# One VectorE operation for the low halves of an expert's weights, GpSimd left with the scatters, SyncE reading its table four values at a time

## The reference

```python
x = hidden_states.reshape(-1, orig_shape[-1])
probs = jax.nn.softmax(x @ gate_w.T, axis=-1)
topk_w, topk_idx = jax.lax.top_k(probs, K)                    # K = 6 of E = 64
topk_w = topk_w / jnp.sum(topk_w, axis=-1, keepdims=True)
combine = jnp.sum(jax.nn.one_hot(topk_idx, E, dtype=x.dtype) * topk_w[..., None], axis=1)
h = jax.nn.silu(jnp.einsum('th,eih->tei', x, experts_w1))     # 256 -> 176
y = jnp.einsum('tei,ehi->teh', h, experts_w2)                 # 176 -> 256
routed_out = jnp.einsum('teh,te->th', y, combine)
...
shared_out = jax.nn.silu(g) * u @ shared_down.T
return (routed_out + shared_out).reshape(orig_shape)
```

## Time and profile before

| | before |
|---|---|
| median of 3 executions | 1873.75 us (1868.09 to 1883.21) |
| the profiled execution | 1885.33 us, of which the span from the first to the last instruction is 1883.4 us |
| TensorE busy | 1558.3 us (83%) |
| VectorE busy | 1331.7 us (71%) |
| ScalarE busy | 922.6 us (49%) |
| GpSimd busy | 911.4 us (48%) |
| mean granted TensorE clock | 0.899 of full speed |
| GpSimd, `outputs<-hsw,x_rows` (L1358) | 160 times, 243.1 us |
| GpSimd, `ew_lo<-ew,ew_hi` (L1294) | 160 times, 154.7 us |
| VectorE, `ew_lo<-ew,ew_hi` (L875) | 160 times, 108.4 us |

### The profile page before, as it was taken

The page is one execution under the profiler, slowest core; times in us unless marked ns, Lnnn a source line. Parts: engine busy times, 40 slices in busy tenths (PEclk is TensorE's granted clock), DMA queues, the critical chain, the costliest instruction groups (busy, mean ns, idle before and its releaser), DMA issues. The chain is left out here.

```text
span 1883.4 us, 33921 instructions
## 1 busy us (share of the span) xinstructions
PE 1558.3 (83%) x9484; PEld 1165.7 (62%) x9484; DVE 1331.7 (71%) x2125; ACT 922.6 (49%) x1696; POOL 911.4 (48%) x714
## 2 busy tenths in 40 slices
PE   6689998699996899986999978716299999999931
PEld 5466665566664666654666648404198888878820
DVE  3568887588886688875888855503567777777767
ACT  3465554555554655546555533101076666666610
POOL 0334433434343444334344410566378999989920
PEclk8799999999998999998999985757599999999965
DMA  4012221022220112210221200334388888888744
GB/s 141 0 43 63 62 67 34 8 64 61 67 58 9 42 59 67 67 33 0 67 67 58 61 3 1 138 117 157 96 252 250 246 245 248 247 241 234 209 165 161
DMA packets 111029, 198.16 MB, mean 105 GB/s; under 512 B 17481, under 2 KB 63063, under 8 KB 110816
## 3 DMA queue, kind: packets, MB, share of 16 engines
q1 hardware_dynamic: 98656, 171.75, 30.9%
q0 software_dynamic: 12288, 25.41, 3.7%
HBM read 160.96 MB, written 44.50 MB: 109 GB/s over the span
## 5 line engine op out<-in xcount | busy, mean ns | idle before, releaser
L1307 POOL TENSOR_TENSOR ssq<-ssq,ysq 128x512 f32<-128x512 f32 x128 | 164.4, 1284 | 460.9 <-ACT ysq L759 460.9
L963 DVE SCALAR_TENSOR_TENSOR e<-bank,scal,e 128x511 f32<-128x511 f32 (+2 forms) x384 | 287.5, 749 | 54.3 <-ACT e L754 18.9
L1358 POOL DMA_INDIRECT outputs<-hsw,x_rows x160 | 243.1, 1519 | 33.3 <-issue 28.5
L461 PE MATMUL bank<-e,wn 128*128 128x512 f32 x512 | 252.8, 617 | 0.0
L386 PE MATMUL bank<-h_hi,wi_hi 128*128 x512 | 237.2, 463 | 18.8 <-POOL wi_lo L1294 14.6
L388 PE MATMUL bank<-h_hi,wi_lo 128*128 x512 | 204.9, 400 | 0.0
L387 PE MATMUL bank<-h_lo,wi_hi 128*128 x512 | 202.2, 395 | 0.0
L875 DVE TENSOR_TENSOR hid_lo_rows<-hid_rows,hid_hi_rows 88x256 fp32r<-88x256 f32 x160 | 120.9, 756 | 113.6 <-ACT hid_hi_rows L705 111.3
L754 ACT ACTIVATE e<-bank,scal 128x512 f32<-128x512 f32 x128 | 99.7, 779 | 199.0 <-PE bank L388 199.0
L1294 POOL TENSOR_TENSOR wi_lo<-wi,wi_hi 128x512 fp32r<-128x512 f32 x128 | 165.5, 1293 | 52.7 <-ACT wi_hi L705 52.7
L386 PE MATMUL bank<-hw_hi,ew_hi 128*88 128x128 f32 x640 | 161.0, 256 | 22.3 <-POOL ew_lo L1294 5.9
(11 more groups left out here) (245 smaller groups left out, 3764.3 us busy)
## 6 DMA issues: line engine op xcount, KB each, us to landing
ew<-expert_w SPq DMA_DIRECT2D x160, 432.0 KB
wi<-in_w SPq DMA_DIRECT2D x128, 256.0 KB, 2.7
x_rows<-grouped SPq DMA_DIRECT2D x160, 130.0 KB
wo<-out_w SPq DMA_DIRECT2D x128, 128.0 KB, 2.4
got<-outputs SPq DMA_DIRECT2D x16, 768.0 KB, 4.3
grouped<-zeros_out SPq DMA_DIRECT2D x65, 130.0 KB
outputs<-hsw,x_rows POOLq DMA_INDIRECT x160
x_all<-x_t SPq DMA_DIRECT2D x4, 512.0 KB, 8.6
```

What stands on the lines that cost most here:

```text
L461: i = mm(p_out[k][:, :], wn[:, par, k * P:(k + 1) * P], y[:, par, :], start=do_out == "first", stop=do_out == "last")
L963: v.scalar_tensor_tensor(dst[:, d:], src[:, 0:SEQ - d], taps(TAPS - 1 - d), dst[:, d:], ALU.mult, ALU.add).then_inc(S[done], 1)
L1307: g_.tensor_tensor(ssq[:, :], ssq[:, :], ysq[:, :], ALU.add).then_inc(S["ssq_done"], 1)
L1358: g_.indirect_dma_start(outputs, bass.IndirectOffsetOnAxis(x_rows[:, i % XD, EMB:EMB + 1].bitcast(U32), 0), y_rows[:, i % YD, :], None, bo ...
```

## The change

Three edits, all around the expert loop.

- VectorE makes the low part of all 864 columns of tile i+1 in one operation (`weights_low`), at the place in its order where it made 512 of them. It signals `w_lo`; the semaphore `w2_lo` is gone, and so is TensorE's wait for it in `second`. Before the loop, `weights_low(0)` comes ahead of `rows_in(0)` and `rows_in(1)` instead of behind them.
- GpSimd's `first_weights` is gone. It issues the 160 scatters, each as soon as its rows are copied.
- SyncE reads four values of a table with one load. In the loop it handles four tiles at a time: eight values are read first, then the transfers are issued. Before tile 4 the order of the first transfers is four loads of rows, then four of weights.

```diff
-            def load_weights(i):
-
-                e = sp.value_load(owner_no[0:1, i:i + 1], min_val=0, max_val=EXPERTS - 1)
+            def load_weights(i, e):
+
                 sp.wait_ge(S["w_lo"], START["w_lo"] + i - 3)
-                sp.wait_ge(S["w2_lo"], START["w2_lo"] + i - 3)
                 sp.dma_start(ew[:, i % DEEP, :], expert_w[bass.ds(e, 1), :, :].rearrange("a p n -> p (a n)"))\
                     .then_inc(S[f"w_in{i % DEEP}"], 16)
...
+            def four(table, i, top):
+
+                return nc.values_load_multi_w_load_instructions(table[0:1, i:i + 4], engines=[mybir.EngineType.SP],
+                                                                min_val=0, max_val=top)[1]
+
             sp.wait_ge(S["fill_rows"], 1)
-            for e in range(EXPERTS):
-                row = sp.value_load(fill_row[0:1, e:e + 1], min_val=0, max_val=SPARE - P)
-                sp.dma_start(grouped_rows[bass.ds(row, P), :], zeros_out[:, :]).then_inc(S["xs_zero"], 16)
+            for e in range(0, EXPERTS, 4):
+                for row in four(fill_row, e, SPARE - P):
+                    sp.dma_start(grouped_rows[bass.ds(row, P), :], zeros_out[:, :]).then_inc(S["xs_zero"], 16)
...
-            for i in range(DEEP, ETILES):
-                load_weights(i)
-                if i + 2 < ETILES:
-                    load_rows(i + 2)
+            early = four(first_row, 0, SPARE)
+            for i in range(DEEP):
+                load_rows(i, early[i])
+            owners = four(owner_no, 0, EXPERTS - 1)
+            for i in range(DEEP):
+                load_weights(i, owners[i])
+            for n in range(DEEP, ETILES, 4):
+                rows, owners = four(first_row, n, SPARE), four(owner_no, n, EXPERTS - 1)
+                load_rows(n, rows[0])
+                load_rows(n + 1, rows[1])
+                load_weights(n, owners[0])
+                load_rows(n + 2, rows[2])
+                load_weights(n + 1, owners[1])
+                load_rows(n + 3, rows[3])
+                load_weights(n + 2, owners[2])
+                load_weights(n + 3, owners[3])
...
             def second(i):
                 r = i % DEEP
                 pe.wait_ge(S["row_done"], START["row_done"] + i - 1)
-                pe.wait_ge(S["w2_lo"], START["w2_lo"] + i + 1)
                 pe.wait_ge(S["hid_lo"], START["hid_lo"] + i + 1)
...
-            def second_weights(i):
+            def weights_low(i):
                 dve.wait_ge(S["w_hi"], i + 1)
-                w = slice(W1_COLS, ECOLS)
-                low(ew_lo[:, i % DEEP, w], ew[:, i % DEEP, w], ew_hi[:, i % DEEP, w]).then_inc(S["w2_lo"], 1)
+                low(ew_lo[:, i % DEEP, :], ew[:, i % DEEP, :], ew_hi[:, i % DEEP, :]).then_inc(S["w_lo"], 1)
...
+            weights_low(0)
             rows_in(0)
             rows_in(1)
-            second_weights(0)
             for i in range(ETILES):
...
                 low(hid_lo[0:IHALF, i % 2, :], hid[0:IHALF, i % 2, :], hid_hi[0:IHALF, i % 2, :]).then_inc(S["hid_lo"], 1)
                 if i + 1 < ETILES:
-                    second_weights(i + 1)
+                    weights_low(i + 1)
                 if i:
                     row_done(i - 1)
...
-            def first_weights(i):
-                pool.wait_ge(S["w_hi"], i + 1)
-                w = slice(0, W1_COLS)
-                low(ew_lo[:, i % DEEP, w], ew[:, i % DEEP, w], ew_hi[:, i % DEEP, w]).then_inc(S["w_lo"], 1)
-
...
             for i in range(ETILES):
-                first_weights(i)
-                if i >= 3:
-                    scatter(i - 3)
-            for i in range(ETILES - 3, ETILES):
                 scatter(i)
```

More of the change, by code:

```diff
@@ L89, in program @@
                  "x_turned": 4, "x_lo": 2, "first_mm": 4, "second_mm": 4, "w_lo": 4, "hid_silu": 2, "hid_lo": 2,
-                 "row_done": 2, "w2_lo": 4, "acc_chain": 7, "acc_turned": 2, "final": 3}
+                 "row_done": 2, "acc_chain": 7, "acc_turned": 2, "final": 3}
         def sb(name, shape, dt=F32, on=ctx):
@@ L276, in program @@
             inner inner_silu prod weighted hw_hi hw_lo expert_mm result stored zero_set
-            w2_lo x_turned x_hi x_lo w_in0 w_in1 w_in2 w_in3 w_hi w_lo
+            x_turned x_hi x_lo w_in0 w_in1 w_in2 w_in3 w_hi w_lo
             first_mm hid_silu hid_hi hid_lo second_mm row_done
@@ L333, in _, with load_rows @@
                     load_out(b, PAIRS - 2 + par, par)
-            def load_weights(i):
-                e = sp.value_load(owner_no[0:1, i:i + 1], min_val=0, max_val=EXPERTS - 1)
+            def load_weights(i, e):
                 sp.wait_ge(S["w_lo"], START["w_lo"] + i - 3)
-                sp.wait_ge(S["w2_lo"], START["w2_lo"] + i - 3)
                 sp.dma_start(ew[:, i % DEEP, :], expert_w[bass.ds(e, 1), :, :].rearrange("a p n -> p (a n)"))\
                     .then_inc(S[f"w_in{i % DEEP}"], 16)
-            def load_rows(i):
-                row = sp.value_load(first_row[0:1, i:i + 1], min_val=0, max_val=SPARE)
+            def load_rows(i, row):
                 if i >= XD:
@@ L357, in _ @@
                 sp.wait_ge(S[f"sent{q}"], 16 * TOP_K * GTILES // HD)
-            for i in range(DEEP + 2):
-                load_rows(i)
-                if i < DEEP:
-                    load_weights(i)
-            for i in range(DEEP, ETILES):
-                load_weights(i)
-                if i + 2 < ETILES:
-                    load_rows(i + 2)
+            early = four(first_row, 0, SPARE)
[14 more added lines that the diff above has]
+                load_weights(n + 3, owners[3])
             for j in range(ETILES - YD, ETILES):
```

## The result

The changed kernel takes **2022.62 us** (median of 4, 2020.91 to 2025.59) against 1873.64: a ratio of 1.079, 95% interval 1.074 to 1.084. It is 149 us slower; 2038 was forecast. The profiled execution took 2021.26 us with a span of 2019.5.

What follows compares the result with a forecast made beforehand. The prediction took GpSimd to set the pace, TensorE close behind. 152.2 + 1.05 + 1.5 + 0 = +154.8 us on 1885.33 gave 2040 us, or 2029 on the median; the forecast was 2038 us, range 2010 to 2075.

Steps and rivals of the forecast that it cites:

- What bounds the kernel now: Expert loop: GpSimd sets the pace at 2.74 us a tile, TensorE close behind at 2.38 us.
- The loop of waits: Expert loop: first product, Silu, high part, hid_lo, 864 columns, next first product; 3.68 us a tile, +152.2 us over 159 steps.
- its six terms: Pieces of one tile's chain of waits in the expert loop: 1.25 + 0.47 + 0.45 + 0.34 + 1.05 + 0.12 us.
- The sixth: Expert loop: from the end of a VectorE result to the TensorE weight load that waited for it, 0.12 us.
- The start of the loop: Expert loop's start: first 864 columns uncovered, +1.05 us; one or two tiles at the low TensorE clock, +1.5 us.
- SyncE's part at 0: SyncE's fills and loop loads: four-value reads win or cost nothing, between -5 and +5 us for the fills.
- The base: Whole kernel: the profiled 1885.33 us as starting time, held likelier than the median, 1873.75 us.
- the sum, 154.8 us: Whole kernel: the added time of all parts, 152.2 + 1.05 + 1.5 + 0 us, giving 2040 us on the profiled execution.
- the faster rival: Expert loop: 864 columns ready before TensorE asks, 2.38 us a tile, -54.5 us, 1829 us; chance 0.03.
- the forecast's own range: Whole kernel: 2012 to 2062 us, from the lower base with 3.62 us a tile to 3.80 us a tile; chance 0.84.
- the clock: Rival, expert loop: TensorE's clock falls; with half of the tiles low, +79 us, 2117 us; chance 0.07.
- The meeting with GpSimd: Rival, expert loop: the scatter reaches into hid_lo, 0.39 us a tile, +62 us, 2100 us; chance 0.04.

Runs made afterwards that it cites:

- e1_ahead: The changed kernel with VectorE's 864 columns of tile i+1 ahead of the wait for tile i's high part, not behind hid_lo: 1827.82 us, 0.977 of the kernel before.
- e4_split: The changed kernel with the 864 columns cut in two operations at the same place, 352 first, then 512 with their own semaphore: 1932.08 us, 1.031 of the kernel before.
- e5_load: The changed kernel with one more VectorE operation per tile, 512 columns that nobody reads, behind hw_lo: 2022.51 us, 1.081 of the kernel before.
- e9: The kernel before, unchanged, run again for a second profile: 1866.59 us.
- e2: The kernel before with SyncE's part of the change alone, waiting for w2_lo as well: 1871.44 us, 0.998 of the kernel before.
- e3: The changed kernel with SyncE's old code, one value per read and the old order: 2038.03 us, 1.088 of the kernel before.
- e7: The kernel of e1_ahead without the two matmuls per tile whose result nobody reads: 1821.14 us, 0.973 of the kernel before.
- e10: The kernel of e1_ahead with SyncE's old code, one table value per read: 1807.91 us, 0.975 of the kernel before, in a later group of measurements.
- e11: The kernel of e7 with the 864 columns of tile i+1 also ahead of hw_lo of tile i+2: 1777.92 us, 0.959 of the kernel before.
- e6: The changed kernel with the 64 zero fills moved behind the waits for GpSimd's sends: 2077.0 us in one execution.

## Why the prediction was right, point by point

**What bounds the kernel now**: right. With GpSimd's operation gone and the order kept open, the tile falls to TensorE's 2.38 us (e1_ahead), as in the early part of the loop.

**The loop of waits**: right in mechanism and nearly in size, 3.62 us against 3.68. e1_ahead cuts it, e4_split shortens it by the expected amount, e5_load shows that VectorE's load is no part of it. Five of its six terms were right within 0.01 us, the unseen operation included (1.05). The sixth was mis-sized: from VectorE's end to TensorE took 0.05 us and not 0.12. The row taken for it was one in which the weight load's idle time was put down to "issue"; GpSimd's own handover of `ew_lo` (its end at 1602.81, the load at 1602.86) was nearer to the case. With the one step in 16 that is longer the mean is 3.638, which makes 145.5 us instead of 152.2.

**The start of the loop**: the terms +1.05 and +1.5 us were too high. From SyncE's first load of rows to the first `hid_lo` it takes 1358.89 - 1344.49 = 14.40 us, and in e9, the kernel before with an early start, 1351.65 - 1337.24 = 14.41 us, so both measure nothing. The first 864 columns lay beside the 24 matmuls that TensorE runs ahead of the loop (1346.80 to 1355.29) and whose result nobody reads, and the granted clock was 1.00 from the first tile on (windows from 1355 us). In the profile before, TensorE had stood idle for 14.30 us ahead of the loop, which the late start had caused, and the first tile ran at a granted clock of 0.50 (1365 to 1368 us); in e9 the wait there was 0.81 us and the clock 1.00 (1349 to 1351 us). The cover that the prediction counted on for the reordered transfers, VectorE's older work, was gone (it ended at 1337.5, before the first load), and the new order still cost nothing against e9.

**SyncE's part at 0**: right within what can be measured for the kernel before (e2). For the changed kernel it was some 15 us in e3's measurement, by way of the late start, and this was not foreseen. I had looked for what waits for the fills, and not for what the waits beside them did to VectorE's work ahead of the loop, which had lasted until 1364.7 in that profile.

**The base**: this choice was wrong. I held the kernel before's spread for the length of its early regime and took the profiled 1885.33 us as the base. e9 shows an early regime of the same length in a shorter execution, and a loop that starts 17 us earlier. On the two profiled executions the sum, 154.8 us, was 18.9 too long: 6.7 in the loop, 2.55 in the start's terms, and 9.7 for the earlier start, which it did not have. With the median as base, the prediction's own sum gives 2029 us. The profile that a sum is made on should have been compared with the median by its parts, as far as the rows allow. Two slips of arithmetic changed nothing: the faster rival is 1885.33 - 54.5 = 1831 us and not 1829, and the ends of the forecast's own range come to 2019 and 2059 us from the terms that it names, and not 2012 and 2062.

**The rivals**: the clock did not fall. TensorE was busy for 0.72 of the loop, with a gap of 1.25 us on its weight loads in each tile, and the granted clock was 1.00 all the same. The meeting with GpSimd is gone (0.42 us in all 160 `hid_lo`), but by 0.14 us and not 0.6, since the scatter starts 0.8 us after the copy and not 0.3. This rival's price was wrong as well, and the miss did not matter: in e4_split and e1_ahead the scatter and `hid_lo` lie beside each other and `hid_lo` takes 0.41 to 0.45 us. The rows held this already: the `hid_lo` of 0.42 us at 1400.58, read as undisturbed, lies inside the scatter from 1400.34 to 1401.34. The 0.81 and 1.58 us belong to GpSimd's subtraction, `ew_lo`, which the change removes: both end 0.29 us after it (it ends at 1602.81 and 1418.50). The faster rival was what the change would have done with its call two lines higher.

## What to carry to other kernels

Before work is moved to an engine with room, write down what that engine waits for ahead of the new place, and follow it around: if the moved result is needed for the next step's first product and the engine waits there for this step's result, the steps can no longer overlap, however low the busy shares are (here 2022.6 us, with no engine busy for over 0.72 of the loop, against 1827.8 with the call two lines higher). The sum of such a loop, taken from the gaps of the old timeline, came within 2% here. And if a kernel's times fall in two groups, find out to which one the profiled execution belongs before its own time is used as a base.

## What the runs showed of the hardware that was not expected

- How long a scatter takes depends on what VectorE is doing when it starts. The scatter's instruction on GpSimd takes 0.98 or 0.99 us in e4_split, where VectorE is idle at its start (106 of the 107 between 1370 and 1700 us) or runs the copy (one), though `hid_lo` follows 0.5 us later. When the 864 columns are running at its start, it ends 0.84 to 0.89 us after them, and so takes up to 1.8 us (e1, e7, e10 and e11, same stretch). `hid_lo` beside a scatter alone takes 0.41 to 0.45 us in these five runs and 0.42 to 0.49 in the kernel before; the 0.81 us of the earlier trace rows needed GpSimd's own arithmetic (the 139 beside its `ew_lo` take 0.52 to 1.91 us).
- The granted clock stayed at 1.00 from 1360 to 1940 us in the changed kernel, while TensorE was idle for 28% of the time, in pieces of about 1 us.
- 64 fills of 130 KB take 55.7 us behind GpSimd's sends (e6) and 58.8 us beside them (e11), both with four values per read. In the runs in which ScalarE waits, they take 110.1 to 120.7 us with four values per read (six runs) and 129.3 to 141.9 us with one (three runs).
- ScalarE waits 38.9 to 80.6 us in the shared expert for something that the trace does not name, in all profiles but those of e10 and e11, which have no such wait. Where such a wait falls into that stage's second half it can start the loop up to 17 us late (e9, e3); its cause stays open.
